# A residual added one step later in two attentions, and where and when the unit keys are loaded and made

## The reference

```
def _L0_xattn_ref(q, k, v):              # layer 2 is the same, times gamma
    qk = jnp.einsum('bdm,bdn->bmn', qh, kh) * scale
    sm = jax.nn.softmax(qk, axis=-1)
    ret = jnp.einsum('bmn,bcn->bcm', sm, vh)
def _L1_xattn_ref(q, k, v):
    qn = _l2norm(qh, axis=-2)
    kn = _l2norm(kh, axis=-2)            # the "unit keys"
    qk = ALPHA * jnp.einsum('bhdq,bhdk->bhqk', qn, kn)
...
x = x + _L0_xattn_ref(_layernorm(x, axis=-1), ctx_2048, ctx_2048)
x = x + _L0_ffn_ref(_layernorm(x, axis=-1), L0_ffn_w1, L0_ffn_w2)   # ternary weights, 8-bit activations
x = x + _L1_xattn_ref(_layernorm(x, axis=-1), ctx_2048, ctx_2048)
...
```

## Time and profile before

| what | us |
|---|---|
| median of 3 runs | 1389.22 |
| lowest, highest | 1385.08, 1393.35 |
| the profiled execution | 1382.25 |
| its span | 1380.5 |
| layer 0 attention, about 0 to 201 in the span | 201 |
| ternary feed-forward, to 276.5 | 75.5 |
| layer 1 attention, to 398 | 121.5 |
| layer 1 mixture, to 522.4 | 124.4 |
| layer 2 attention, to 692 | 169.6 |
| busy over the span: PE, DVE, ACT, POOL | 1110.6, 664.3, 638.4, 551.0 |

### The profile page before, as it was taken

The page is one execution under the profiler, slowest core; times in us unless marked ns, Lnnn a source line. Parts: engine busy times, 40 slices in busy tenths (PEclk is TensorE's granted clock), DMA queues, the critical chain, the costliest instruction groups (busy, mean ns, idle before and its releaser), DMA issues. The chain is left out here.

```text
span 1380.5 us, 19222 instructions
## 1 busy us (share of the span) xinstructions
PE 1110.6 (80%) x6655; PEld 792.0 (57%) x6656; DVE 664.3 (48%) x1377; ACT 638.4 (46%) x1009; POOL 551.0 (40%) x624
## 2 busy tenths in 40 slices
PE   2877754359779994978659999999976668999997
PEld 1434421334368882544348888888733456888886
DVE  6645547761363337766373333333377852333333
ACT  5544447749734433644434334434364433433342
POOL 5145520000226652221226666666411125666663
PEclk9967765779969995887869999999998869999999
DMA  6632222057513314331104334333110003333331
GB/s 207 194 101 83 91 90 56 1 129 198 137 49 121 113 61 125 114 109 60 47 29 134 117 106 167 119 118 109 42 28 1 1 24 125 120 117 106 106 119 60
DMA packets 65956, 132.43 MB, mean 96 GB/s; under 512 B 10123, under 2 KB 33099, under 8 KB 65254
## 3 DMA queue, kind: packets, MB, share of 16 engines
q1 hardware_dynamic: 62758, 127.04, 30.2%
q10 hardware_dynamic: 2112, 4.19, 0.9%
q0 software_dynamic: 1024, 0.41, 0.1%
HBM read 115.55 MB, written 15.45 MB: 95 GB/s over the span
## 5 line engine op out<-in xcount | busy, mean ns | idle before, releaser
L1406 POOL TENSOR_TENSOR f_hid<-f_gated,f_coef 128x512 f32<-128x512 f32 x152 | 224.0, 1474 | 161.2 <-DVE f_gated L1437 149.5
L1437 DVE TENSOR_TENSOR f_gated<-f_act_g,f_p_u 128x512 f32<-128x512 f32 x152 | 104.4, 687 | 261.9 <-PE f_p_u L1269 258.3
L912 DVE TENSOR_REDUCE a_maxes<-a_p_max 128x2 f32<-128x512 f32 x256 | 161.5, 683 | 108.2 <-PE a_p_max L677 108.1
L791 ACT ACTIVATE a_probs<-a_p_sc 128x1024 f32<-128x1024 f32 x192 | 188.5, 1018 | 42.1 <-PE a_p_sc L710 36.6
L1346 ACT ACTIVATE f_hid_hi<-f_hid 128x512 fp32r<-128x512 f32 x152 | 96.2, 633 | 206.6 <-POOL f_hid L1406 206.5
L1441 DVE TENSOR_TENSOR f_hid_lo<-f_hid,f_hid_hi 128x512 fp32r<-128x512 f32 x152 | 105.9, 697 | 150.7 <-ACT f_hid_hi L1346 150.3
L1341 ACT ACTIVATE f_act_g<-f_p_g 128x512 f32<-128x512 f32 x152 | 90.8, 597 | 162.6 <-PE f_p_g L1269 162.6
L677 PE MATMUL a_p_max<-a_k,a_q 72*128 72x256 bf16 x512 | 105.7, 338 | 45.8 <-DMA a_q<-q_parts 37.8
L710 PE MATMUL a_p_sc<-a_q,a_k 75*128 75x256 bf16 (+1 forms) x768 | 128.5, 300 | 9.8 <-ACT a_probs L791 5.1
L1282 PE MATMUL f_p_y<-f_hid_hi,f_down_hi 128*128 128x512 f32 x304 | 119.7, 394 | 6.9 <-issue 6.9
L730 PE MATMUL a_p_out<-a_probs,all_v 128*32 128x256 f32 x1536 | 124.2, 444 | 1.2 <-ACT a_probs L791 1.2
(11 more groups left out here) (285 smaller groups left out, 1695.4 us busy)
## 6 DMA issues: line engine op xcount, KB each, us to landing
f_w<-in_w SPq DMA_DIRECT2D x76, 384.0 KB, 3.5
f_coef<-coef SPq DMA_DIRECT2D x51, 512.0 KB, 3.7
a_q<-q_parts SPq DMA_DIRECT2D x48, 288.0 KB
a_k<-k_plain SPq DMA_DIRECT2D x96, 96.0 KB
outs<-a_out SPq DMA_DIRECT2D x48, 128.0 KB, 1.7
a_whole<-outs SPq DMA_DIRECT2D x48, 128.0 KB, 2.5
q_parts<-a_q_part SPq DMA_DIRECT2D x48, 96.0 KB, 3.2
a_k<-k_unit SPq DMA_DIRECT2D x24, 192.0 KB
```

The source lines that it names most:

```text
L791: nc.scalar.activation(probs[b % 2][:, 2 * pair:2 * pair + 2, :, :].rearrange("p h t d -> p h (t d)"), p_sc[pair % 2][:], ACT.Exp, scale=s ...
L912: nc.vector.tensor_reduce(maxes[b % 3][:, :, h], p_max[:, n % 3, :].rearrange("p (t d) -> p t d", t=NK), axis=AX.X, op=ALU.max, negate=Tru ...
L1406: nc.gpsimd.tensor_tensor(hid[c][:], gated[c][:], coef[slot(t, 2)][:, c * 512:(c + 1) * 512], ALU.mult).then_inc(hid_done, 1)
L1437: nc.vector.tensor_tensor(gated[c][:], act_g[c][:], p_u[c][:], ALU.mult).then_inc(gated_done, 1)
```

## The change

1. `add_tile(i)` comes on POOL at b = 8 + 2i instead of 6 + 2i, in layers 0 and 2.
2. The unit keys are loaded over ACT's queue at b = 1, their squares summed in steps 4 to 7 (two groups each), the clamp is after maximum 84; the root, the inverse and the 40 operations of `split` move into the ternary stage, and SP's stores there wait for each part.
3. The first layer's large loads of x and of the context (896 KB each) go over ACT's queue instead of SP's, and the first load of v is issued later on ACT.

```diff
--- before
+++ after
@@ UnitKeys, store_unit_keys
-    def load(self, sp, a):
-        sp.dma_start(self.keys[:], a["ctx_heads"]).then_inc(self.loaded, 16)
+    def load(self, act, a):
+        act.dma_start(self.keys[:], a["ctx_heads"]).then_inc(self.loaded, 16)
+
+    def ready(self, sp, part, c):
+        sp.wait_ge((self.hi_ready, self.mid_ready, self.lo_ready)[part], c + 1)
...
-    for part in range(3):
-        for c in range(CH):
+    for c in range(CH):
+        for part in range(3):
+            m.unit_keys.ready(sp, part, c)
@@ attention, sync
                     sp.dma_start(keys[:, 0:1, :], a["ctx"][:, 0:1, :]).then_inc(keys_loaded[0], 16)
-                    sp.dma_start(m.x[:, 1:NI, :], a["x"][:, 1:NI, :]).then_inc(m.x_loaded[1], 16)
-                    sp.dma_start(keys[:, 1:NI, :], a["ctx"][:, 1:NI, :]).then_inc(keys_loaded[1], 16)
...
-                    if layer == 0 and b == 2:
-                        unit_keys.load(sp, a)
@@ attention, scalar
                 if layer == 0:
+                    act.dma_start(m.x[:, 1:NI, :], a["x"][:, 1:NI, :]).then_inc(m.x_loaded[1], 16)
+                    act.dma_start(keys[:, 1:NI, :], a["ctx"][:, 1:NI, :]).then_inc(keys_loaded[1], 16)
                     act.wait_ge(keys_loaded[0], 16)
...
                     act.wait_ge(keys_loaded[1], 16)
-                    load_v(0)
...
                     norm.apply_by_act(5)
+                    load_v(0)
...
-                        if layer == 0 and b == 5:
-                            unit_keys.root(act)
+                        if layer == 0 and b == 1:
+                            unit_keys.load(act, a)
@@ attention, vector
-                            if n == 7 * HEADS + 4:
+                            if n == 10 * HEADS + 4:
                                 unit_keys.clamp(dve)
-                            if n == 8 * HEADS:
-                                unit_keys.invert(dve)
@@ attention, gpsimd
-                        if b >= 6 and b % 2 == 0 and b // 2 - 3 < 4:
-                            add_tile(b // 2 - 3)
+                        if b >= 8 and b % 2 == 0:
+                            add_tile(b // 2 - 4)
                         if b + 2 < B:
                             split_max(b + 2)
-                        if layer == 0 and b < 5:
-                            for c in range(3 * (b - 2), min(3 * (b - 1), CH)):
+                        if layer == 0 and 4 <= b < 8:
+                            for c in range(2 * (b - 4), 2 * (b - 3)):
                                 unit_keys.add_square(pool, c)
-                        if layer == 0 and 6 <= b < 6 + CH:
-                            if b == 6:
-                                for g, (lo, hi) in enumerate(CUTS):
-                                    pool.wait_ge(k_stored[g], 16 * (hi - lo))
-                            for what in range(5):
-                                unit_keys.split(pool, one, what, b - 6)
                     for i in range(4, LATE):
                         add_tile(i)
+                if layer == 0:
+                    for g, (lo, hi) in enumerate(CUTS):
+                        pool.wait_ge(k_stored[g], 16 * (hi - lo))
@@ ternary_feed_forward
                     nc.gpsimd.memset(ones[:], 1.0).then_inc(ones_set, 1)
+                    pool.wait_ge(ones_set, 1)
+                    for c in range(CH):
+                        for what in range(5):
+                            m.unit_keys.split(pool, ones, what, c)
...
                     norm.scalar(act)
+                    m.unit_keys.root(act)
...
                     link(v.tensor_reduce(largest[:], m.xn[:], axis=AX.X, op=ALU.max, apply_absolute_value=True))
+                    m.unit_keys.invert(dve)
```

5 lines of the change are left out of this document (4 added, 1 removed).

## The result

The changed kernel took 1336.38 us (median of 4 runs, 1323.36 to 1342.53), the kernel before 1387.15 us (4 runs): a ratio of 0.9618, interval 0.9535 to 0.9701. That is 51 us less. The profiled execution took 1334.24 us against 1382.25, 48.0 less where the sum of the prediction had 63.4.

| piece | before | after | difference | forecast |
|---|---|---|---|---|
| start to store of out(2), layer 0 | 63.23 | 65.94 | +2.7 | -1.5 |
| out(2) to out(12), layer 0 | 113.11 | 80.09 | -33.0 | -48.6 + 1.5 |
| out(12) to the ternary stage | 24.81 | 21.60 | -3.2 | 0 |
| ternary stage | 75.54 | 84.32 | +8.8 | +14.4 |
| its end to out(4) of layer 2 | 311.34 | 313.89 | +2.5 | 0 |

The account below looks back on a forecast made before the run. Bound: TensorE idling in even steps for POOL's split, late behind DVE's inverse, then running at low clock. Terms -29.2 - 48.6 + 1.5 - 1.5 + 0.9 + 13.5 = -63.4 from 1382.25 gave 1318.9, forecast 1326 us on the median's scale; range 1308 to 1346.

Parts of the forecast that it names:

- rival C: Layer 0 falls short: loads come late while 2 MB run over ACT's queue, +14 instead of +1.5, 1338.5 us; chance 0.16.
- Layer 2: Residual one step later: eight steps at 6.52 us, 52.2 instead of 81.4, so -29.2 us.
- Layer 0's steps: Residual later and unit keys out: ten steps from out(2) take 64.5 us instead of 113.1, so -48.6.
- part 2b: Layer 0, unit keys' load on ACT's queue behind v's second MB: between nothing and +14 us, taken as +1.5.
- part 2a: Unit keys' work out of layer 0's steps; two square groups stay in steps 4 to 7; with the residual, -48.6 us.
- The head: SP's first key store no longer waits behind 1.8 MB: -1.5 us, half of a gain of up to 3.0.
- The ternary stage: Reciprocal on DVE, +0.9 us, and DVE's instructions held up by POOL's 40 operations, +13.5.
- Rival B: Ternary stage: POOL and DVE do not hold each other up, the 13.5 us go, 1312.5 us; chance 0.15.
- D: Head: the small first loads share with the large ones, +2.6 us instead of -1.5, 1330 us; chance 0.12.
- E: Even steps keep their hole, POOL's own work being too long; attentions gain nothing, ternary stage pays 14.4, 1403.6 us; chance 0.02.
- F: L1033's wait goes but other links hold the steps, so gain and cost cancel, 1389 us; chance 0.03.

Follow-up runs that it names:

- v in pieces: Changed kernel with v's second to fourth MB loaded in twelve 256 KB pieces, one a step, instead of 1 MB in steps 1, 5 and 9; 1317.97 us.
- first try with the keys in the steps: Changed kernel with v in pieces, large first loads on SP, unit keys loaded in four pieces, root, inverse and splits in layer 0's steps; 1316.29 us.

## Why the prediction was right, and where it was not

The time came out 10 us above the forecast of 1326, inside the range and nearest to rival C's 1338.5. The mechanism that carried most of the sum was the one that the runs showed: with the residual moved alone, the wait for the inverse is gone and the kernel takes 54.6 us less than the runs beside it. Point by point:

- **Layer 2**, -29.2: measured -29.2.
- **Layer 0's steps**, -48.6: the floor of 64.5 us was right as a floor (64.68 with v in pieces) and wrong as a forecast, since the steps took 80.1, 15.6 more. The step that failed is part 2b, "+1.5, near the lower end, since the loads are due one or two steps after issue". For the loads that counted this was false: q of batch 6 was wanted 5.7 us after its issue, less than a step, and TensorE got on only at 69.97, 9.7 us after it, with v's second megabyte and the unit keys beside it. That hole cost 8.6 us. The other 7.0 had no term at all, for 2b priced the unit keys' load alone: v's third and fourth megabyte, which were there before, made the small load of the turned maxima late (it took 6.5 and 7.3 us and was wanted 4.6 and 6.4 after its issue). The row of 6.2 us had said that such a load uses that time up, and part 2a's sentence on the squares that they leave it about 4 us; the two stand a paragraph apart, and I did not add them. So that 15.6 lies near the upper bound of 14 is partly luck. In the kernel before, these small loads were as late beside v (5.9 us from 90.48, 6.7 from 139.57) without a hole of their own; I take it that the holes in the even steps covered them. With the residual alone moved, the fourth megabyte's hole appeared.
- **The head**, -1.5: +2.7 to out(2). I took the gain; the first loads do share, and what I had set as the bound of the loss (+2.6) is what came. With these loads back on SP's queue 1.5 us of the first store's delay went away. The rule of the Trainium skill, page DMA: Bandwidth & Descriptors, section on queues, rings and completion order, that the engines take turns between rings with work, agrees with the landings of 4.1 and 6.3 us against 2.5.
- **The tail of layer 0**, not in the sum: -3.2, the granted clock and not work saved. The run with the residual alone has 21.6 us too, but two kernels with the residual moved have 24.9 and the long rows of matmuls again. In layer 2 it is the same: 14.2 us from out(12) to out(15) instead of 15.8, and 15.8 again with the residual alone.
- **The ternary stage**, +14.4: +8.8, of which 7.55 fall with the splits. The number of instructions held was nearly right (32 in the trace, 33 in the count) and the price too high: 0.38 us instead of 0.5 for each rounding of a tile (with what TensorE's wait absorbs 5.8 instead of 9), 1.0 in all for the three long ones instead of 1.5, and 1.7 in the scales instead of 3. The 0.9 for the reciprocal can't be read, since the stage varies by as much.
- **The rest**, nothing in the sum, +5.8. The part behind layer 1's start varies by 12 us between profiled executions of one and the same code, so no effect of the change can be read there, nor in a difference of that size between two medians. Between the changed kernel and v in pieces 6.7 us of it lie behind layer 2, where the granted clock of TensorE in two stretches of 60 us, from 972.6 us and from 955.5, is 0.83 and 0.69 in the one and 0.89 and 0.74 in the other.

Had 2b been at its upper bound and the head at its own, the sum would have been 63.4 - 12.5 - 4.1 = 46.8 us of gain; measured 48.0. That they agree so well is luck: the steps and the head fell short by 18.3 us and the rest by 5.8, and the ternary stage and the tail gave 8.8 back.

Rival B fell with the run without splits. C and D both came true, C against the reason that I had given for its low chance, and the ternary stage's lower price and the tail hid 8.8 us of them in the total: a time inside the range is not yet a sum that is right. E and F fell; for the parts 2 and 3 alone, F's sentence, gain and cost cancel, is what happened (7.4 gained, 7.6 paid).

## What to carry to other kernels

When a wait is removed from a loop, list the transfers that the wait had covered, above all the smallest with the shortest due time, and add up for it: how late it is issued, when it is wanted, and what large transfer is under way on another queue meanwhile. Cut large background loads into a piece a step. Work moved off a busy stage onto an "idle" engine is priced in the stage where it lands, by what runs beside it there; run each part of a change alone, since here one line of it held the whole gain.

## What the runs showed of the hardware that I had not expected

- A tensor_tensor on DVE with both inputs in SBUF can be held beside POOL: 128 x 8, 0.65 us against 0.17 without the splits (L1640), where L235 had spoken against it. That is the rule of the Trainium skill, page GPSIMD Engine Reference, section Key points, which I had set aside. Not each of them is held: L1639, just ahead of it, took 0.17. One of 128 x 256 took 0.83 instead of 0.42 beside POOL's residual (L941, first try with the keys in the steps, 155.69 us).
- Holding goes both ways: beside DVE's roundings of 128 x 2048, POOL's operations of 0.61 to 0.67 us took 1.47 to 1.53.
- A load of 12 KB on POOL's queue landed in 6.5 and 7.3 us beside v's third and fourth megabyte on ACT's queue and in 8.3 beside the unit keys' (one step later), in 4.3 to 4.7 with v in pieces of 256 KB (84.50 to 97.17 us), and in 2.0 with nothing large beside it.
- A hole of 1.91 us cost its step 4.7 us, since 6 us at the granted clock of 0.50 followed; the one of 3.96 cost 8.6.
- The same code with the same waits of 0.65 and 0.77 us ran at a granted clock of 1.00 in one kernel and fell to 0.50 in another, 3.2 us in a tail of 22. A stage that nobody edited can differ by that.
